# Two megakernel layers on one core: multiplications of a constant added ahead of seven kinds of TensorE groups

## The reference, cut to what matters

```python
x = x + 0.5 * _L0_ffn_ref(_layernorm(x), w_gate, w_up, w_down)      # FP4 quantised, hidden 704
x = x + _L0_attn_ref(_layernorm(x), Wv, Wk, bk, Wq, bq, Wo)         # decaying linear attention, blocks of 128
x = x + 0.5 * _L0_ffn_ref(_layernorm(x), w_gate, w_up, w_down)
x = x + 0.5 * _L1_ffn_ref(_layernorm(x), gamma_x, gamma_slot, slot_embeds, w1, w2)   # soft mixture of 8x128 slots
x = x + _L1_attn_ref(_layernorm(x), wq, aq, bq, ...)                # causal softmax attention, 16 heads, LoRA
x = x + 0.5 * _L1_ffn_ref(_layernorm(x), gamma_x, gamma_slot, slot_embeds, w1, w2)
```

## Time and profile before

| | |
|---|---|
| median of 3 runs | 2934.41 us (2932.08 to 2935.42) |
| the profiled execution | 2929.66 us, of which 2927.6 us span from the first to the last instruction |
| busy: PE, DVE, ACT, POOL | 83%, 72%, 56%, 37% of the span |
| mean granted TensorE clock | 0.935 of full speed |

### The profile page before, as it was taken

One profiled execution on the slowest core, in us unless ns is written; L12 is line 12 of the kernel. 1 busy time (PEld: TensorE's weight loads), 2 busy tenths in 40 slices (PEclk: granted clock), 3 DMA queues, 4 the chain that ended last, 5 costly groups with the idle time before them and its releaser, 6 DMA issues.

```text
span 2927.6 us, 56018 instructions
## 1 busy us (share of the span) xinstructions
PE 2429.8 (83%) x23228; PEld 1846.8 (63%) x23228; DVE 2108.1 (72%) x3530; ACT 1625.4 (56%) x2761; POOL 1096.1 (37%) x791
## 2 busy tenths in 40 slices
PE   1677777778888988889889889889898888898888
PEld 0445555555666766657567666667666667677666
DVE  6599999889898886777877777776786765343432
ACT  2244544454765757365566556574656566556554
POOL 0144544444352443244443526262525252222112
PEclk9799998899999999989898999999989999999999
DMA  4000000000000000000000000000000000000000
GB/s 153 17 1 1 1 1 1 1 1 1 1 1 1 1 1 1 23 13 12 11 14 2 23 2 23 2 23 2 23 9 21 12 2 8 8 8 1 8 8 8
DMA packets 34572, 32.96 MB, mean 11 GB/s; under 512 B 7377, under 2 KB 33681, under 8 KB 34321
## 3 DMA queue, kind: packets, MB, share of 16 engines
q1 hardware_dynamic: 34320, 29.40, 3.1%
HBM read 12.34 MB, written 4.19 MB: 6 GB/s over the span
## 4 chain that ended last, share of the span: by engine, by line
PE 44%; DVE 17%; ACT 6%; issue 4%; POOL 4%; SPq 1%; DMA 1%; POOLq 0%; DVEq 0%; ACTq 0%
PE psum L623 11%; PE psum L625 10%; PE psum L624 10%; PE psum L629 3%; PE psum L1055 2%; DVE a1pr L1771 2%; PE psum L1057 2%; PE psum L1056 2%; POOL f1hT L2042 2%; PE psum L906 1%; PE psum L959 1%; DVE f1d L1882 1%; DVE a1c L1789 1%; PE psum L936 1%; DVE f1e L1886 1%
## 5 line engine op out<-in xcount | busy, mean ns | idle before, releaser
L2042 POOL TENSOR_TENSOR f1hT<-f1g,f1hT 128x512 f16<-128x512 f32 x256 | 311.7, 1224 | 677.1 <-ACT f1hT L1422 676.6
L2029 POOL TENSOR_TENSOR a1pr<-a1PT,a1pr 128x1024 f16<-128x1024 f32 (+1 forms) x176 | 350.3, 1992 | 334.9 <-DVE a1pr L1771 334.9
L623 PE MATMUL psum<-f1sl,f1w1h 128*128 128x256 f16 x1024 | 290.4, 284 | 30.7 <-DVE f1pr L1929 16.6
L623 PE MATMUL psum<-f1w2h,f1hT 128*128 128x256 f16 x1024 | 282.4, 276 | 17.0 <-POOL f1hT L2042 15.2
L624 PE MATMUL psum<-f1sl,f1w1h 128*128 128x256 f16 x1024 | 290.0, 283 | 0.0
L625 PE MATMUL psum<-f1sl,f1w1l 128*128 128x256 f16 x1024 | 289.7, 283 | 0.0
L624 PE MATMUL psum<-f1w2l,f1hT 128*128 128x256 f16 x1024 | 281.6, 275 | 0.0
L625 PE MATMUL psum<-f1w2h,f1hT 128*128 128x256 f16 x1024 | 281.4, 275 | 0.0
L1748 DVE TENSOR_REDUCE a1nm<-psum 128x2 f32<-128x768 f32 (+3 forms) x176 | 198.1, 1125 | 79.1 <-PE psum L886 77.7
L2006 POOL TENSOR_TENSOR f0hT<-f0Y,f0hT 128x512 f16<-128x512 f32 (+1 forms) x128 | 139.6, 1105 | 181.4 <-ACT f0Y L1214 181.4
L1771 DVE CAST a1pr<-a1PT 128x1024 f16<-128x1024 f32 (+1 forms) x176 | 156.0, 891 | 69.5 <-ACT a1PT L1318 49.5
(11 more groups left out here) (335 smaller groups left out, 7502.1 us busy)
## 6 DMA issues: line engine op xcount, KB each, us to landing
a1Q<-a1st SPq DMA_DIRECT2D x96, 64.0 KB, 2.6
a1K<-a1st SPq DMA_DIRECT2D x96, 64.0 KB, 2.5
x<-in_L_attn_x SPq DMA_DIRECT2D x8, 512.0 KB, 8.8
out<-x SPq DMA_DIRECT2D x8, 512.0 KB, 3.0
wslot<-in_L_ffn_w SPq DMA_DIRECT2D x1, 1024.0 KB, 7.5
wraw<-in_L_ffn_w SPq DMA_DIRECT2D x1, 1024.0 KB, 5.7
wslot<-in_L_ffn_slot_embeds SPq DMA_DIRECT2D x1, 1024.0 KB, 8.2
a1Q<-a1mr SPq DMA_DIRECT2D x64, 4.0 KB, 1.7
```

The lines of the kernel that those rows point to most:

```text
L623: e.matmul(out, lh, rh, start=start, stop=False)
L2029: e.tensor_tensor(a1["pr"][:, i % 2, 1, :, 0:w], a1["PT"][:, i % 2, :, 0:w], a1["pr"][:, i % 2, 0, :, 0:w], ALU.subtract).then_inc(s["a1_pl"])
L2042: e.tensor_tensor(hT1[:, 1, 2 * hp:2 * hp + 2, :], gg[:, hp % 2, :, :], hT1[:, 0, 2 * hp:2 * hp + 2, :], ALU.subtract).then_inc(s["f1_hl"])
```

## The change

A function `warm(v, n)` is added. It emits n matmuls of the 128x128 identity `idb` (bf16) with 512 columns of the constant `neg` into the bank v. Their result is overwritten by the group that follows, whose first matmul starts afresh. It emits nothing while `rehearse` runs, so the order of all other pieces stays as it was. At the seven places above, the bank is now taken first, then `warm(v, 4)` stands, and then the waits for the operands. Two of the places (f1mt and f1_slots2) do so only for j >= 12; f0_gate only for the first token tile of an item, a0_blocks for the first block, a1_front for the first projection, f1_slots2 for i = 0.

```diff
+            def warm(v, n):
+
+                if q.notes is None:
+                    q.wait_ge("w_k", 2)
+                    for i in range(n):
+                        e.matmul(v, idb[:, :], neg[:, 0:4 * P], start=True, stop=True)
...
                         up, hf = divmod(n, 2)
+                        v = bank(n)
                         if n == 0:
+                            if t == 0:
+                                warm(v, 4)
                             q.wait_ge("w_l", W_L["tail", 1])
                             q.wait_ge("f0_xl", 2 * f + t // 2 + 1)
                             q.wait_ge("f0_hT", 2 * (ft - 2))
-                        v = bank(n)[:, 0:FH]
+                        v = v[:, 0:FH]
...
                     yield S + 3.5 + 0.8 * k
+                    v = bank(4 + k)
+                    if k == 0:
+                        warm(v, 4)
                     q.wait_ge("a0_xn", 4 * b + 4)
-                    v = bank(4 + k)
...
                     yield N + 2.5
+                    v = bank(5)
+                    if n == 0:
+                        warm(v, 4)
+                    v = v[:, 0:P]
                     q.wait_ge("a0_ql", 2 * b + 2)
                     q.wait_ge("a0_kl", 2 * b + 2)
-                    v = bank(5)[:, 0:P]
...
                     yield S + 9.0 + 1.6 * i
+                    v = bank(2)
+                    if i == 0:
+                        warm(v, 4)
                     q.wait_ge("w_l", W_L["a1w", 3])
                     q.wait_ge("a1_xl", 2 * b + 2)
...
-                    q.wait_ge("f1_u", j + 1)
                     bk = 4 + k
                     v = bank(bk)
+                    if k == 0:
+                        warm(v, 4)
+                    q.wait_ge("f1_u", j + 1)
...
                 yield S + 34.5
+                v = bank(4)
+                if j >= B + 4:
+                    warm(v, 4)
                 q.wait_ge("f1_mt", j + 1)
-                v = bank(4)
...
                         yield E + 5.6 + 2.5 * i
+                        bk = 4 + i
+                        v = bank(bk)
+                        if i == 0 and j >= B + 4:
+                            warm(v, 4)
                         q.wait_ge("f1_nl", j + 1)
                         q.wait_ge("f1_el", n + 1)
```

More of the change, by code:

```diff
@@ L862, in a1_front @@
                     q.wait_ge(f"a1_{'qk'[k_]}{1 - c}", 96 * (b + c))
-                    v = bank(2)
                     W, cs = w1a["qk"[k_]], slice(c * P, (c + 1) * P)
@@ L1051, in f1_slots2 @@
                         es = slice(i * P, (i + 1) * P)
-                        bk = 4 + i
-                        v = bank(bk)
                         for t in range(NT):
```

## The result

The change takes 2936.49 us (median of 12 runs, 2931.20 to 2941.29), the kernel before 2932.55 (12 runs, 2926.83 to 2935.42): a ratio of 1.0018, 95% interval 1.0011 to 1.0026, about 5 us more. The forecast was 2959, with a range from 2941 to 2976. It was too high by 20 us. The forecast had called anything within 0.2% no change; 0.18% lies within that.

A forecast was written before the change was run, and what follows sets the result against it. VectorE was taken to lead until 700 us, TensorE to bound the last stretch from 2360. Cost 36.6 us less 11.4 of clock gives 25, on the median 2934.4: 2959 us, range 2941 to 2976.

The forecast's parts named there:

- The places and their waits: At the 76 places, 304 new matmuls leave 49.2 us of new TensorE time that no operand wait hides.
- What the clock gives back: In thin TensorE stretches the new matmuls prevent some clock drops: 11.4 us returned, 5.8 of it in the last part.
- the clock comes back at the same moment as before: Where TensorE would have worked on anyway at half clock, four new matmuls therefore still cost 0.86 us.
- a mean clock of 0.945: Sign of being right: TensorE's mean clock rises from 0.935 to about 0.945.
- What of it reaches the end: Share of new TensorE time passed on: 4.3 us by 700 us, 12.1 in the middle, 20.2 last; 36.6 together.
- Nothing is removed and nothing moves to another queue: The change only adds four matmuls, 0.86 us at full clock, at each place.
- late operand: At 32 places of a0_front, a0_blocks and f1_front, 21 waits hide most; 1.9 us overhangs, 9.5 for the other 11.
- bank is the operand: At 24 places of f0_gate and a1_front the bank's release is the operand's writing, so all is added: 20.6 us.
- bank last, last four items: At 20 f1mt and slot-sum places the bank comes last or TensorE doesn't wait, so all is added: 17.2 us.
- The clock pays for all: Rival: all 14 low stretches vanish, returning 45.3 us against 36.6, so 9 us faster, 2926; 6 in 100.
- The waits swallow it: Rival: later waits absorb half the last stretch's cost and a third of the middle's; 5 us more, 2939; 8 in 100.
- No clock: Rival: no clock comes back and all the added time is passed on, 2984; 10 in 100.

The follow-up runs named there:

- e13_thin: The change with its 304 matmuls multiplying only 16 of the 128 rows; ratio 1.0104 to the kernel before.
- e15_free: Kernel before with late-coming waits written first, plus matmuls into unused bank 0 ahead of f1mt and the first three slot groups in the last four items; ratio 0.9964.
- c0_null: The kernel before, unchanged, measured once more against itself; ratio 0.9993.
- e9_others: Kernel before with the bank taken first at f0_gate, a0_front, a0_blocks, a1_front and f1_front's transposes, no matmuls added; ratio 1.0001 to the kernel before.
- e1_late: The change with its matmuls kept only at the 32 places of a0_front, a0_blocks and f1_front, bank first everywhere; ratio 0.9965 to the kernel before.
- e7_mixed: The change with four full matmuls at the 32 late-operand places and one of 16 columns at the other 44; ratio 0.9963 to the kernel before.
- e10_apart: Kernel before with all 304 matmuls added but the old order of waits kept; ratio 1.0029 to the kernel before.
- e14_late: Kernel before with late-coming waits written first, plus four matmuls at the 32 places of a0_front, a0_blocks and f1_front; ratio 0.9963.
- e16_both: Kernel before with late-coming waits written first, four matmuls at the 32 late-operand places and bank 0 matmuls in the last four items; ratio 0.9958.
- e5_order: The change without any added matmul, only the bank taken ahead of the operand waits at the seven places; ratio 0.9964 to the kernel before.
- e8_slots: Kernel before with the bank taken first only in f1_slots2 and at f1mt, no matmuls added; ratio 0.9971 to the kernel before.
- e2_gate: The change with its matmuls kept only at the 24 places of f0_gate and a1_front, bank first everywhere; ratio 0.9989 to the kernel before.
- e3_tail: The change with its matmuls kept only at the 20 f1mt and slot-sum places of the last four items, bank first everywhere; ratio 1.0011 to the kernel before.
- e12_latefirst: Kernel before with the wait that comes late written first at seven kinds of groups, nothing added; ratio 0.9953 to the kernel before.

## Why the prediction was wrong

**The places and their waits: right.** What the sum's first part reads from the trace came: 304 matmuls of line 636, the waits on lines 1882 and 1911 taken over by it, shorter waits for a0xh, a0kT and f1u, slot groups that start later than before.

**An account by parts.** A trace's clock record gives the time at 1.2 GHz, and its matmuls the time within it in which TensorE worked on anything but the added matmuls. The last column says how much time the part took more than in the kernel before, by the start of the same VectorE instruction (all traces have 3530 of them); in the first row it counts from the program's start. One profile each, in us:

| part | before: low time, work in it | the change | e13_thin | longer: the change, e13_thin |
|---|---|---|---|---|
| 100 to 700 | 102.8, 78.8 | 88.9, 72.7 | 99.0, 78.9 | -0.6, 7.2 |
| 700 to 2360 | 198.0, 164.0 | 157.3, 130.6 | 167.2, 136.6 | -3.6, 0.5 |
| from 2360 on | 69.2, 42.2 | 44.7, 19.3 | 83.9, 44.8 | 10.3, 24.8 |
| all three | 370.0, 285.0 | 290.9, 222.6 | 350.1, 260.3 | 6.1, 32.5 |

Half the work that left the low time is an estimate of what the clock gave back. It takes for granted that all of it reaches the end, which in e15_free it did not. c0_null, the same program once more, has 290.7 us of work in the low time and e9_others, which takes as long (1.0001), 265.5, so a total can be off by 10 us of time.

**"What the clock gives back": the step that failed.** Forecast 11.4 us, as 1.2, 4.4 and 5.8 us in the three parts; the estimate from the change is 3.0, 16.7 and 11.4 us, 31 in all (21 if the low time of e9_others stands for before). That is the whole 20 us by which the forecast was off, give or take ten, and most of it lies in the middle. The mean clock (0.949 over the twelve runs too) agrees that it was well above 11: 0.065 below full before is 381 us at the lower level, 0.051 after is 299, 82 less; at the density of the stretches in the earlier trace rows, (34.3 + 56.3) / (58.1 + 81.9) = 0.65 us of work in each us, half of which is won, 26 us.

Two things in the forecast's working were wrong. It looked at 14 low stretches of 140.0 us that have a place near them, and of these mostly at the beginning, while the trace had 380 us of low time. And it took for granted that "the clock comes back at the same moment as before". At the first slot groups of the last four items the low stretches lasted 13.7, 13.7, 10.2 and 13.7 us before (13.7 and three of 10.3 in c0_null), and 10.2, 6.8, 6.8 and 6.8 in the change: beside the items' f1mt transposes they began later and ended earlier (2632.8 to 2639.6 instead of 2629.7 to 2643.4 at j = 13), although the bank is held there as before. In e13_thin, with the matmuls at the same places, they lasted 17.1, 13.7, 13.7 and 13.7. In the middle the return goes with the late operands: the low time from 700 to 2360 us was 143 to 167 us in the six traces with four full matmuls there (the change, e1_late, e7_mixed, e10_apart, e14_late, e16_both), and 173 to 208 in the eleven with none or the small ones. The forecast held its own warning: a mean clock of 0.945, which it named as the sign of being right, is 59 us less at the lower level, worth 19 us and not 11.

**"What of it reaches the end": about right, to some 10 us.** Forecast 36.6 us without the clock, as 4.3, 12.1 and 20.2. What each part took more plus the estimate for the clock gives 2.4, 13.1 and 21.7 for the change, 37 in all, and 7.2, 14.2 and 23.5 for e13_thin, 45 in all. Both include what the moved waits gain. e13_thin by itself is 30.5 us slower than before (0.0104 of 2932), but it had bought some clock too. The full matmuls against the thin ones gain 25.2 us by the ratios (1.0104 less 1.0018), of which half the difference in work, 19 us, is accounted for; the rest is open.

**A term that was not in the sum: the order of the waits.** "Nothing is removed and nothing moves to another queue" overlooked the waits. I had seen in the order that the bank's wait went ahead of the operand's, and charged nothing and credited nothing. That no instruction was removed held; but it is worth 0.36% alone (e5_order), of which 0.29% in f1_slots2 and f1mt (e8_slots), and about 0.1% in the change (e10_apart). 0.09 us at each of the 56 groups, if all of them waited, would be 5 us. The rest can be the clock in the last part: work in the low time fell there from 42.2 and 46.7 us (before, c0_null) to 33.3 (e8_slots), half of which is 4.5 to 6.7 us. That the short stretches at the third slot group go with the order of the waits is shown by thirteen traces; how an earlier start of 0.09 us does it is not. Why the waits are worth 10.6 us alone and 3 beside the matmuls is open; the likeliest reason is that both remove the same low time, since the change has none at the third slot groups either.

**By kinds of places,** against e5_order (0.9964), which has the same waits:

| places | raw cost forecast | forecast at the end | measured, give or take 4 us |
|---|---|---|---|
| late operand (e1_late) | 11.4 | 7 less some clock | 0.3 |
| bank is the operand (e2_gate) | 20.6 | 12 less some clock | 7.3 |
| bank last, last four items (e3_tail) | 17.2 | 17.2 - 5.8 = 11.4 | 13.8 |
| all (the change) | 49.2 | 25 | 15.8 |

The third line was forecast well, the second within its error. At the late operands the four cost nothing, as a whole: they won 6 us ahead of the last items (2402.3 against 2408.4) and lost 4 in them (421.4 against 417.8). e14_late against e12_latefirst, the same pair with more waits turned, does the same (5 and 3 us). The three parts add up to 21.4, but with the error of four ratios in it this can't be told from the 15.8 of all together.

**Rivals.** The clock pays for all (2926): no. Its 45 us were for 14 stretches; from all of the low time some 20 to 30 came back. It named the right mechanism, and it deserved a term between it and mine. The Trainium skill's rule that stood beside it (TensorE: Matmul & The Clock Gate, section on HAM oscillation) holds for the slots' start, which was slow still at 2636.8; 30.6 of the 58.1 us of low time stayed. The waits swallow it (2939): nearest in time, and the result is within the noise as it said, but for the wrong reason, since e13_thin shows that most of the cost arrives. No clock: no.

## What to carry to other kernels

Where a group waits for several semaphores, find out which wait the compiler puts on the instruction itself (here the one that the code asks for first) and write the one that comes last there. Look at this before adding any work: here it was worth 0.36 to 0.47%, and no version with added matmuls on top of it was faster. Added matmuls cost nothing where TensorE waits for an operand and holds the bank already, but even there they gained nothing. Where the bank is what is waited for they delay the group by their full length, and the clock returned less than that. When a change touches the clock, forecast the mean granted clock first and work out the return from the whole program's low time as well as stretch by stretch: the two must agree. Half the work in the low time is only an estimate of it: look for the next wait behind, which may take the won time back, as VectorE's order did in e15_free.

## What the runs showed of the hardware

- A matmul that carries the awaited semaphore itself started 0.05 us behind the signal (e5_order), one behind an instruction that waited for it 0.14 us. Over the whole trace of before, the medians were 0.046 us (some 250 waits) and 0.136 us (some 100 waits).
- 512-column matmuls of 16 rows last as long as ones of 128 rows (0.374 and 0.378 us recorded), but with them the mean granted clock was 0.941 and not 0.949, and the low stretches of the last part summed to 68.4 us and not 30.6. In this kernel the number of rows mattered to the granted clock, and not to the matmul's own length.
- More time at 2.4 GHz need not be less time: over all their runs e12_latefirst, e15_free and e16_both had mean clocks of 0.939, 0.945 and 0.952, with ratios of 0.9953, 0.9964 and 0.9958, which can't be told apart.
